# Products that nobody reads in four waits of TensorE

## The reference, cut to what matters

```
xn = layernorm(x)
out = x + attention(xn) + ffn(xn)

attention: causal over all 1024 rows, 8 heads of 128 over 2 key/value heads,
           keys and values through a latent of 32
ffn:       6 layers, each: local attention (16 heads of 64, window 32, rotary,
           normalised queries and keys), then a gated feed-forward (gelu)
```

## Time and profile before

| | |
|---|---|
| median of three runs | 1732.24 us |
| the profiled execution | 1739.99 us |
| its span | 1738.2 us |
| PE busy | 1593.9 us, 92% |
| DVE / ACT / POOL busy | 1357.6 / 1278.8 / 1291.7 us (78 / 74 / 74%) |
| mean granted clock | 0.982 |

### The profile page before, as it was taken

The page is one execution under the profiler, slowest core; times in us unless marked ns, Lnnn a source line. Parts: engine busy times, 40 slices in busy tenths (PEclk is TensorE's granted clock), DMA queues, the critical chain, the costliest instruction groups (busy, mean ns, idle before and its releaser), DMA issues.

```text
span 1738.2 us, 70552 instructions
## 1 busy us (share of the span) xinstructions
PE 1593.9 (92%) x29272; PEld 1219.8 (70%) x29272; DVE 1357.6 (78%) x1875; ACT 1278.8 (74%) x1888; POOL 1291.7 (74%) x1227
## 2 busy tenths in 40 slices
PE   6999978899999999899999899998999999999996
PEld 4777856667667767667776677776677767767774
DVE  5677857788778888888888788887888877878873
ACT  3788846677777777678778777776886777788773
POOL 2222159788978888888898888889788988888871
PEclk8999989899999999999999999999999999999997
DMA  5211212433324433334333344333243333333331
GB/s 146 67 48 38 54 25 69 127 86 89 96 67 101 105 86 88 82 80 127 83 88 91 79 104 107 83 93 93 67 128 83 86 84 82 82 77 78 81 80 42
DMA packets 127629, 146.51 MB, mean 84 GB/s; under 512 B 58448, under 2 KB 71504, under 8 KB 125776
## 3 DMA queue, kind: packets, MB, share of 16 engines
q1 hardware_dynamic: 127312, 141.98, 33.2%
HBM read 25.47 MB, written 1.05 MB: 15 GB/s over the span
## 4 chain that ended last, share of the span: by engine, by line
PE 65%; ACT 10%; DVE 9%; issue 8%; POOL 4%; SPq 2%; DMA 1%; DVEq 0%; ACTq 0%; POOLq 0%
PE banks L1260 40%; PE banks L1546 8%; PE banks L1501 7%; PE banks L1606 6%; PE banks L1392 4%; ACT vst L839 3%; ACT banks L854 2%; DVE arena L1102 2%; ACT arena L796 1%; POOL prob L576 1%; SPq L414 1%; DVE small L1131 1%; DVE small L1137 1%; DVE small L1149 1%; DVE arena L1097 1%
## 5 line engine op out<-in xcount | busy, mean ns | idle before, releaser
L581 POOL TENSOR_TENSOR arena<-arena 128x1024 f32<-128x1024 f32 x96 | 230.2, 2398 | 76.0 <-DVE arena L1102 75.9
L1149 DVE TENSOR_REDUCE small<-banks 128x16 f32<-128x1024 f32 x96 | 117.6, 1225 | 205.0 <-PE banks L1546 204.8
L839 ACT ACTIVATE vst<-banks 128x1024 f32<-128x1024 f32 x192 | 196.5, 1024 | 83.5 <-PE banks L1260 70.9
L1097 DVE TENSOR_TENSOR arena<-banks,tabs 128x1024 f32<-128x1024 f32 x192 | 233.5, 1216 | 20.8 <-ACT arena L796 19.3
L1102 DVE TENSOR_TENSOR arena<-banks,tabs 128x1024 f32<-128x1024 f32 x192 | 233.2, 1215 | 0.0
L586 POOL TENSOR_TENSOR arena<-arena 128x1024 f32<-128x1024 f32 x96 | 228.4, 2379 | 0.0
L576 POOL TENSOR_TENSOR prob<-prob,small 128x1024 f32<-128x1024 f32 x96 | 184.1, 1918 | 26.7 <-DVE small L1139 26.4
L1546 PEld LDWEIGHTS banks<-arena 64*32 64x32 f32 x12288 | 134.7, 106 | 98.0 <-issue 95.6
L1546 PE MATMUL banks<-arena 64*32 64x64 f32 x12288 | 166.9, 226 | 39.5 <-ACT banks L854 24.4
L1260 PE MATMUL banks<-qkH,xsH 128*128 128x512 f32 x384 | 178.5, 465 | 25.8 <-DVE arena L1102 13.8
L1606 PE MATMUL banks<-arena 128*32 128x128 f32 x6144 | 190.9, 277 | 0.2 <-issue 0.2
(11 more groups left out here) (146 smaller groups left out, 3746.3 us busy)
## 6 DMA issues: line engine op xcount, KB each, us to landing
arena<-vst SPq DMA_DIRECT2D x1536, 64.0 KB, 2.0
qkraw<-in_wqk_dram SPq DMA_DIRECT2D x6, 1024.0 KB, 5.8
arena<-in_wvo_dram SPq DMA_DIRECT2D x5, 1024.0 KB, 5.4
tabs<-in_tab_dram SPq DMA_DIRECT2D x40, 128.0 KB, 2.5
gq<-w1w SPq DMA_DIRECT2D x64, 64.0 KB, 2.0
lns<-Xt SPq DMA_DIRECT2D x96, 32.0 KB
lns<-Xt SPq DMA_DIRECT2D x96, 31.8 KB
xsH<-w1w SPq DMA_DIRECT2D x32, 64.0 KB, 2.0
```

Of the source, the lines that this page charges most:

```text
L581: pool.tensor_tensor(kc, kc, ks, ALU.add).then_inc(s["k_add"], 1)
L839: act.activation(vst[:, g, :], two(V_BANK), ACT.Copy).then_inc(s[f"v_cp{g}"], 1)
L1097: dve.tensor_tensor(heads(c), heads(two(0)), table(k % NT, kind), ALU.mult).then_inc(s[done], 1)
```

## The change

VectorE fills 640 columns of `arena` with ones as its first instruction, and counts a new semaphore `idle` up. TensorE waits for it and runs five 128x512 products of these columns into bank 2 before it waits for the first weights, and four more behind the first three units of queries and keys, ahead of the first scores. Two further groups read `qkH`, one-pass, and write bank 5: eight between `products(0, 0)` and `products(0, 1)`, and ten behind `shifts(0)` in step G = 1. Nobody reads the results; the next user of each bank overwrites it.

```diff
@@ vector
+            dve.memset(arena[:, 0:P + CH], 1.0).then_inc(s["idle"], 1)
@@ tensor
+            def idle_columns(bank, count):
+                for _ in range(count):
+                    mm(bk(bank), arena[:, 0:P], arena[:, P:P + CH])
+
+            pe.wait_ge(s["idle"], 1)
+            idle_columns(2, 5)
             pe.wait_ge(lat_wq, 32)
...
             for unit in extras[-1][0:3]:
                 unit_in(unit)
+            idle_columns(2, 4)
...
+            def idle_products(bank, count):
+                claim(bank)
+                for _ in range(count):
+                    mm(bk(bank), qkH[:, 0, 0:P], qkH[:, 1, 0:CH])
...
             products(0, 0)
+            idle_products(5, 8)
             products(0, 1)
...
                 if G == 1:
                     shifts(0)
+                    idle_products(5, 10)
                 down_last(chunk_at(G, 13))
```

More of the change, by code:

```diff
@@ L214, in build @@
                   "st_bn st_ag st_eps ln_x0 rs_0 ln_mr gK_lo gQ_lo gL_max gS_max gB_cp gC_cp grec gy_n g_add "
-                  "zeroed gmask ln_x1").split():
+                  "zeroed gmask ln_x1 idle").split():
             s[n] = sem(n)
```

## The result

The changed kernel takes 1723.18 us (median of 6 runs, 1719.2 to 1727.49); the kernel before, run beside it, 1733.72 (6 runs, 1730.62 to 1740.09). The ratio is 0.9927, 95% interval 0.9908 to 0.9945: 0.73% faster, which is 12.7 us; the two medians lie 10.5 us apart. Forecast were 5.7 us. The profiled executions are 1727.49 us (span 1725.7) against 1739.99 (span 1738.2); each is slower than its kernel's median, by 4.3 and 6.3 us.

What follows compares the result with a forecast made beforehand. TensorE, 92% busy, was taken as the bound; 4.7 + 1.0 + 0 = 5.7 us took the profiled 1739.99 to 1734.3, and 7.75 less for the runs' median gave 1726.5 us, range 1721.5 to 1732.

Steps and rivals of the forecast that it cites:

- the third rival: Layers: another offset of all work against waits at the edge saves up to 4.5 us more, total 1722; chance 0.14.
- Layers.* No instruction there changes: Layers behind the passage: no instruction changes, so nothing was added to the forecast sum.
- The memset, nothing: Program start: the 128x640 memset takes 0.6 us on idle VectorE and costs nothing.
- The column's 1.00 before 20 us isn't real: Opening: input products of 1.87 us show 1.2 GHz, although the granted clock column reads 1.00 before 20 us.
- The opening, 4.7: Five and four products up to the first exponentials: higher clock and earlier start gain 4.7 us, bounds -3.0 to +7.
- whatever the opening wins is kept: Behind the opening PE is the bound, 177.5 of 180 us busy from 40 to 220, so its gain stays.
- a drop after the first scores as its lower case, 3.5: Opening: if the clock drops after the first scores, PE idling about 1.5 us between heads, the gain is 3.5 us.
- The eight, 1.0: Passage, between halves of the folded weights: fill the 2.47 us wait, keep the clock up; gain 1.0 us, bounds 0 to 1.2.
- The ten, 0: Before the second key tile: later idle may lower the clock and GpSimd is busy; gain 0, bounds -1.1 to +1.5.
- The clock falls in between: Rival: clock falls during weight products and transposes after the first fill; gain 2.7 us, total 1729.5; chance 0.30.
- The fills overrun: Rival: first fill stays at 1.2 GHz, ends 3.0 us late, the four 5.5 late; total 1738; chance 0.06.
- The clock's total, 5.7 forecast: Opening and passage together: 4.7 + 1.0 + 0 = 5.7 us gained.

Runs made afterwards that it cites:

- the thin kernels: The change with all its 27 added products 8 columns wide instead of 512, against the kernel before: 1729.86 us, 0.9958; in a later session 1729.12 us, 0.9951.
- the nothing at 36: Kernel before plus memset and the opening's nine products 8 columns wide, none in the passage (36 loads and products): 1731.04 us, 0.9995.
- the loss at 144: Kernel before plus 36 products of 32x8 ahead of the first weights (144 loads and products): 1739.76 us, 1.0030.
- the nothing at 248: Kernel before plus 62 products of 32x8, 36 in front and 13 in each passage wait (248 loads and products): 1733.09 us, 1.0003.
- that of the 108: The change plus nine products of 32x8 behind the ten of the passage (108 loads and products): 1726.04 us, 0.9961 of the kernel before.

## Why the prediction was wrong

The size was wrong: 5.7 us were forecast, less than half of the 12.7 of the ratio. The direction was right and the time lies in the range, which had been drawn wide enough for the third rival. The step that failed is the last: "*Layers.* No instruction there changes", with nothing in the sum. No instruction changes there, but 72 more stand ahead of them, and their number alone is worth 8.1 us here: more than all the clock gives (5.4). That is shown by the thin kernels, which keep nothing warm, and by the 18 products in front alone; that it depends on the number, by the nothing at 36, the loss at 144 and the nothing at 248. That it acts through the waits at the block ends of the stream is what their places suggest, which move with the number; it is argued and not shown, since no sum of these waits gives the times. The third rival was close: "another offset of all work against these may save or add some of them", at 1722, with a chance of 0.14 and from the low clock in the earlier trace rows. It named no wait; those that moved are the ones in which the engine waits for no one. I had read the rows with a low clock in the layers and not the "issue" rows beside them.

Term by term:

- *The memset, nothing*: right. It takes 0.59 us, and the kernel with it alone isn't faster (1.0017).
- *The column's 1.00 before 20 us isn't real*: right; the input products took 1.87 before and 0.91 to 0.98 with a burst ahead of them.
- *The opening, 4.7*: mis-sized. The lead of 4.6 at 23.75 us is there. What is left at the first key tile is 2.2 on average, and 1.9 in the time. The step that doesn't hold is "whatever the opening wins is kept": the low clock behind 27 us lasts 13.6 us in two executions, and these keep nothing. Where it lasts 3.4 us or less, most of the lead is kept, although SyncE's copies hold ScalarE and TensorE up there just the same (in the kernel with a wide opening and a thin passage, waits of 0.97 and 1.35 us, no low clock and a lead of 4.1 at the first key tile). The text had a drop after the first scores as its lower case, 3.5; the drop came one wait later and, where it was long, cost all.
- *The eight, 1.0*: the steps are right (wait 0.44, six products in 1.47, VectorE's second reduction 0.97 sooner, at 234.87 in place of 235.84).
- *The ten, 0*: wrong in both of its reasons. The pause behind them, 1.47 us, didn't bring the clock down, and GpSimd, busy for 5.00 of 5 in either kernel, didn't hide the faster TensorE: the passage as a whole gave 2.3 us by the tiles (17.0 against 19.3 on average) and 2.2 to 3.6 in the time, by means or medians, against 1.0.
- *The clock falls in between*: it didn't in this execution, where the clock stayed up through the weights and transposes and until 27.3, and the eight transposes took 1.25 us against 1.95. It did in one of the eight with this opening, that of the 108: low from 12.3 to 15.7 us, so the first scores start at 19.73 in place of 18.95. What followed was not what the rival forecast, for the clock then stayed up, and the first key tile came 3.5 us sooner than before. The Trainium skill, page "TensorE: Matmul & The Clock Gate", section "Part 4: PE-mode transpose", was cited for this rival: transposes don't count as activity in the same way. In the seven others the clock stayed up through them, so it is not borne out here.
- *The fills overrun*: fell. The first fill with the weights behind it ends at 10.4 in place of 11.5. The four end with the copies (the last of head 0 lands at 18.82): the scores of head 0 start without a wait.

The clock's total, 5.7 forecast and 5.4 measured, agrees only because the errors in opening and passage cancel; that is luck.

Open: what a block end costs, and why. The sum of the "issue" waits in the profiled executions doesn't order the kernels: the one with 144 has 14.5 us, like the change with 14.3, and is the slowest; the one with 36 thin ones has the smallest, 12.2, and gains nothing. Both were profiled in executions 6.1 and 3.8 us faster than their medians, so one profile doesn't stand for the kernel here either. Over the 18 profiled executions the span goes more closely with the total time at the low clock (27.5 to 64.7 us, correlation 0.86) than with this sum (0.69). Part of the price may so be the low clock around such a wait, as at 315 us, part the transfers it runs beside; no run tells these apart. Why the clock's low stretch is short in one execution and long in another is open too.

## What to carry over

An added instruction costs or gains not only where it stands: it moves all that follows against places that are fixed in the stream, here about 249.5 loads and products apart. Before a small gain from added or removed instructions is explained, run a twin that has as many at the same places and does nothing (here 8 columns in place of 512), and another count; a gain that the twin shares isn't the mechanism's. And a lead at one place is worth what is left of it at the next engine without slack; read it there, over several executions.

## What the runs showed that was not expected

- Products in front of everything, over before the first weights land, move the program to 0.9965 of its time (72 loads and products) or 1.0030 (144). The waits without a visible cause keep a spacing of about 249.5 loads and products.
- TensorE stands still for up to 2.25 us at such a place ([1.23 <-issue], [2.25 <-issue] above), and for up to 2.46 in the run with the opening alone.
- The granted clock reads 1.00 before its first change, though products of 128x512 take 1.87 us each then and 0.91 to 0.98 at 2.4 GHz.
- The clock's low stretch differs between executions that have the same opening: none, 3.4 us (from 12.3 or from 27.5), or 13.6 us.
